# A decoder layer's projections with another order of loads, fold, keys and queries, and layer norm's last step on ScalarE

## The reference

```
m, v = mean(x), var(x);  xn = (x - m) / sqrt(v + 1e-5)
Q, K, V = xn @ Wq.T + bq, xn @ Wk.T + bk, xn @ Wv.T + bv      # 16 heads of 16
M[h] = shift_weights[h, g - f] for 0 <= g - f < 8, else 0
scores = (gt * (Q W_cross) K + (1 - gt) * Q (M K)) / 4,  gt = sigmoid(gate)
attn = softmax(causal(scores));  x += attn V @ Wo.T + bo
second: cross attention on ctx (4 x 77 x 256), keys ctx @ xWk, values ctx @ xWv
third: a gated feed-forward with integer weights, hidden size 768
```

## Time and profile before

| | us |
|---|---|
| runs, median (3 runs) | 1121.59 (1118.68 to 1123.11) |
| profiled execution | 1129.87 |
| its span | 1128.1 |
| PE busy | 1045.1 |
| DVE busy | 741.7 |
| ACT busy | 562.6 |
| POOL busy | 222.3 |
| mean granted clock of PE, as a share of full | 0.951 |

### The profile page before, as it was taken

How to read it: one execution, slowest core, us unless ns; L and a number is a source line. 1 busy time by engine, 2 the same in 40 slices (tenths; PEclk the granted TensorE clock), 3 DMA queues, 4 the chain that set the end, 5 groups by cost and what they waited for, 6 DMA issues and landing times. The chain is left out here.

```text
span 1128.1 us, 19085 instructions
## 1 busy us (share of the span) xinstructions
PE 1045.1 (93%) x7044; PEld 620.4 (55%) x7092; DVE 741.7 (66%) x1603; ACT 562.6 (50%) x1061; POOL 222.3 (20%) x199
## 2 busy tenths in 40 slices
PE   2888889999999999999999799899898899999997
PEld 2777434444444444444444366444443688888886
DVE  5999887777787778877885266555444555555552
ACT  1445146666666667666766458377655211111110
POOL 6545540000000000000000023201101133333331
PEclk9999779999999999999999899699968899999999
DMA  8259812333444444444400135687971211111101
GB/s 245 104 198 232 260 30 40 64 67 71 74 74 79 81 77 78 81 81 78 78 16 14 25 102 138 144 197 150 220 157 64 74 39 50 51 51 49 44 20 37
DMA packets 87827, 105.27 MB, mean 93 GB/s; under 512 B 14910, under 2 KB 76010, under 8 KB 86199
## 3 DMA queue, kind: packets, MB, share of 16 engines
q1 hardware_dynamic: 85239, 100.90, 38.4%
q10 hardware_dynamic: 2496, 3.16, 1.3%
HBM read 61.80 MB, written 37.06 MB: 88 GB/s over the span
## 5 line engine op out<-in xcount | busy, mean ns | idle before, releaser
L738 DVE TENSOR_REDUCE pm<-bank 128x1 f32<-128x512 f32 (+3 forms) x608 | 356.6, 653 | 87.5 <-PE bank L814 66.7
L786 ACT ACTIVATE prob<-bank 128x512 f32<-128x512 f32 (+1 forms) x608 | 317.4, 583 | 186.0 <-PE bank L830 99.1
L809 PE MATMUL bank<-stk,stq 96*128 96x512 bf16 (+3 forms) x768 | 227.4, 340 | 5.1 <-DVE pm L738 2.9
L826 PE MATMUL bank<-stq,stk 98*128 98x512 bf16 (+3 forms) x768 | 222.4, 330 | 2.6 <-ACT prob L786 0.5
L840 PE MATMUL bank<-prob,va 128*17 128x512 f32 (+3 forms) x1536 | 145.5, 497 | 2.5
L809 PEld LDWEIGHTS bank<-stk,stq 96*128 96x128 bf16 x768 | 68.8, 98 | 136.9 <-DVE pm L738 81.0
L1541 ACT ACTIVATE e_sg<-bank 128x512 f32<-128x512 f32 x48 | 28.7, 598 | 189.3 <-PE bank L135 189.3
L959 POOL TENSOR_TENSOR c_rstd<-c_ve,mhalf 128x4 f32<-128x4 f32 x8 | 8.1, 1011 | 504.9 <-DVE c_ve L128 504.9
L1296 ACT ACTIVATE xprob<-bank 80x512 f32<-80x512 f32 x128 | 72.5, 592 | 69.1 <-PE bank L1336 67.8
L826 PEld LDWEIGHTS bank<-stq,stk 98*128 98x128 bf16 x768 | 69.4, 99 | 44.9 <-ACT prob L786 9.2
L1258 DVE TENSOR_REDUCE xpm<-bank 128x4 f32<-128x320 f32 x128 | 59.0, 488 | 39.1 <-PE bank L1321 37.5
(11 more groups left out here) (172 smaller groups left out, 1403.8 us busy)
## 6 DMA issues: line engine op xcount, KB each, us to landing
qk<-a_parts SPq DMA_DIRECT2D x32, 384.0 KB, 4.4
od<-xu SPq DMA_DIRECT2D x16, 512.0 KB, 4.8
xq<-c_parts SPq DMA_DIRECT2D x16, 384.0 KB, 2.7
xstq<-xq SPq DMA_DIRECT2D x32, 192.0 KB, 4.6
stq<-qk SPq DMA_DIRECT2D x30, 192.0 KB, 4.0
stk<-qk SPq DMA_DIRECT2D x15, 384.0 KB, 6.5
vs<-a_vst SPq DMA_DIRECT2D x8, 544.0 KB, 4.7
oall<-u_out SPq DMA_DIRECT2D x64, 64.0 KB
```

Source lines behind the costliest of these rows:

```text
L738: nc.vector.tensor_reduce(pm[:, k, h0:h0 + hb, r], src[:, 0:hb * w].rearrange("p (h w) -> p h w", h=hb), AX, ALU.max).then_inc(s_mxe, 1)
L786: nc.scalar.activation(prob[:, U % NPS, 0:hb * n], bank[STB[U % NSB]][:, 0:hb * n], ACT.Exp).then_inc(s_ex, 1)
L809: mm = nc.tensor.matmul(dst[:, h * w:(h + 1) * w], stq[i][0:R, half, h0 + h, r * P:(r + 1) * P], stk[i][0:R, h0 + h, k0:k0 + w], start=(h ...
L826: mm = nc.tensor.matmul(dst[:, h * n:(h + 1) * n], stk[i][0:RM, h0 + h, kt * P:(kt + 1) * P], stq[i][0:RM, half, h0 + h, q0:q0 + n], start ...
```

## The change

Five things are moved:
- **Loads.** SP issues x of chunk 0 first, then the gates under a semaphore of their own (`s_gate`), then the other small ones, the context, and bk and bv behind it. ACT issues Wk and Wv ahead of Wq.
- **Before the first chunk.** DVE fills the constant rows of stk (from POOL) and takes the statistics of chunk 0 first, then builds A. PE turns chunk 0 first, then computes the context's products, each in its own bank, then the fold. POOL fills kp, does chunk 0's power, fills vx and takes the weights' low parts before the triangles.
- **Keys in front of queries.** The first pair of products is keys, the second queries, so Wq's low part is due at the third product. The order of the three parts and the place in `qk3` follow.
- **Layer norm's last step.** The mean is taken with its sign reversed, POOL multiplies it by rstd (`negm`), and ACT normalises as scale * x + bias. Its place on ACT is behind middle 3.
- **The bias fold** goes to a spare part of a fold's bank.

```diff
         def qkv_sync(sp):
-            sp.dma_start(wc[:], W_cross.rearrange("(t h) f g -> (h f) t g", t=KT)).then_inc(s_small, 16)
+            sp.dma_start(xres[:, 0], xv[0]).then_inc(ldx[0], 16)
+            for t in range(KT):
+                hs = slice(t * HP, (t + 1) * HP)
...
+                    sp.dma_start(gt[:, t:t + 1],
+                                 gate[hs].rearrange("(h a b) -> h a b", a=1, b=1).to_broadcast([HP, HD, 1])).then_inc(s_gate, 16)
             for t in range(KT):
                 hs = slice(t * HP, (t + 1) * HP)
                 sp.dma_start(sw[:, t, :], shift_w[hs, None, :].to_broadcast([HP, HD, MS])).then_inc(s_small, 16)
...
+            sp.dma_start(wc[:], W_cross.rearrange("(t h) f g -> (h f) t g", t=KT)).then_inc(s_small, 16)
...
-            sp.dma_start(xres[:, 0], xv[0]).then_inc(ldx[0], 16)
...
+            nc.gpsimd.memset(kp[:], 0.0).then_inc(s_con, 1)
+            power1(g, 0)
+            nc.gpsimd.memset(vx[:], 0.0).then_inc(s_con, 1)
+            g.wait_ge(s_con, 2)
+            nc.gpsimd.memset(vx[0:S2, :, :, HD:VW], 1.0).then_inc(s_con, 1)
+            weight_low(n_k, wk, 0)
+            weight_low(n_v, wv, 1)
...
-            power1(g, 0)
-            weight_low(n_k, wk, 0)
-            weight_low(n_v, wv, 1)
+            power1(g, 1)
...
-            self_constants(g, 0, 2)
-            power1(g, 1)
...
             nc.gpsimd.tensor_tensor(rstd[:, c % 2], ve[:, c % 2], mhalf[:], ALU.pow).then_inc(s_pow, 1)
+            g.wait_ge(s_pow, c + 1)
+            nc.gpsimd.tensor_tensor(negm[:, c % 2], mom[:, c % 2, 0], rstd[:, c % 2], ALU.mult).then_inc(s_nm, 1)
...
             nc.vector.memset(vst[:].rearrange("p u g j d h -> p (u g j) d h")[:, :, HD], 1.0)
+            for i in range(2):
+                nc.vector.memset(stk[i][R:RM], -1.0).then_inc(s_set, 1)
+            stats1(0)
             v.wait_ge(s_a, 1)
...
-            stats1(0)
-            normalise1(0)
-            for k in range(KT):
-                v.wait_ge(s_wqh, k + 1)
-                nc.vector.tensor_tensor(wq[:, 1, k], bank[FOLD[k]][:, 0:D], wq[:, 0, k].bitcast(F32),
-                                        ALU.subtract).then_inc(s_wl, 1)
             turned_low(0)
             stats1(1)
...
-            normalise1(1)
+            for k in range(KT):
+                v.wait_ge(s_wqh, k + 1)
+                nc.vector.tensor_tensor(wq[:, 1, k], bank[FOLD[k]][:, 0:D], wq[:, 0, k].bitcast(F32),
+                                        ALU.subtract).then_inc(s_wl, 1)
...
                 split(c, 2)
                 split(c, 3)
-                if c + 2 < NCH:
-                    normalise1(c + 2)
...
-            a.wait_ge(s_small, 16 * N_SMALL)
+            a.wait_ge(s_gate, 16 * KT)
             nc.scalar.activation(ge[:], gt[:], ACT.Exp, scale=-1.0).then_inc(s_a, 1)
+
+            def normalise1(c):
+                u = c % 2
+                a.wait_ge(s_nm, c + 1)
+                need(a, s_tr, KT * (c - 1))
+                for j in range(J):
+                    nc.scalar.activation(xn[:, u, j], xres[:, c, j], ACT.Identity, scale=rstd[:, u, j:j + 1],
+                                         bias=negm[:, u, j:j + 1]).then_inc(s_xn, 1)
+
+            normalise1(0)
...
+            a.wait_ge(s_fold, 2)
+            nc.scalar.activation(qkb[:, 1, :], FOLDB, ACT.Identity).then_inc(s_a, 1)
+            for k in range(KT):
+                nc.scalar.activation(wq[:, 0, k], bank[FOLD[k]][:, 0:D], ACT.Identity).then_inc(s_wqh, 1)
+            normalise1(1)
...
                 middle(c, 2)
                 middle(c, 3)
+                if c + 2 < NCH:
+                    normalise1(c + 2)
...
-                if i:
-                    t.wait_ge(s_kp, 1)
...
                     if c == 0 and n == KT:
-                        t.wait_ge(s_kl, 2)
-                    if c == 0 and n == 3:
-                        t.wait_ge(s_vx, 2)
-                    w_ = (wq, wk)[n // KT]
+                        t.wait_ge(s_wl, KT)
+                        t.wait_ge(s_a, 2)
+                    w_ = (wk, wq)[n // KT]
```

More of the change, by code:

```diff
@@ L167, in program @@
         rstd = sb(qkv, "a_rstd", [P, 2, J])
+        negm = sb(qkv, "a_negm", [P, 2, J])
         xn = sb(qkv, "a_xn", [P, 2, J, D])
@@ L179, in program @@
         ldx = sems("a_ldx", NCH)
+        s_gate = sem("a_gate")
         s_small = sem("a_small")
+        s_nm = sem("a_nm")
         s_wq = sem("a_wq")
@@ L216, in program @@
         TB, QKB, VB = (0, 1), (2, 3, 4, 5), (6, 7)
-        FOLD, CTXK, CTXV = (2, 3, 4), (5, 6), (7, 5)
-        N_SMALL = 2 + 2 * KT
+        FOLD, CTXK, CTXV = (4, 5), (6, 7), (2, 3)
+        FOLDB = bank[FOLD[1]][:, D:D + KT]
+        N_SMALL = 2 + KT
         def part_at(n, part):
-            return part if n < KT else 2 - part
+            return 2 - part if n < KT else part
         def qkv_sync(sp):
-            sp.dma_start(wc[:], W_cross.rearrange("(t h) f g -> (h f) t g", t=KT)).then_inc(s_small, 16)
+            sp.dma_start(xres[:, 0], xv[0]).then_inc(ldx[0], 16)
+            for t in range(KT):
+                hs = slice(t * HP, (t + 1) * HP)
+                with nc.allow_non_contiguous_dma(reason="gates on partitions, a few words"):
+                    sp.dma_start(gt[:, t:t + 1],
+                                 gate[hs].rearrange("(h a b) -> h a b", a=1, b=1).to_broadcast([HP, HD, 1])).then_inc(s_gate, 16)
             for t in range(KT):
@@ L240, in qkv_sync @@
             sp.dma_start(xwv[:], xWv.rearrange("(t p) n -> p t n", p=P)).then_inc(s_ctx, 16)
+            with nc.allow_non_contiguous_dma(reason="biases on partitions, a few hundred words"):
+                sp.dma_start(qkb[:, 0, :], bk.rearrange("(t p) -> p t", p=P)).then_inc(s_wk, 16)
+            sp.dma_start(bv_b[:], bv.rearrange("(a n) -> a n", a=1).to_broadcast([P, D])).then_inc(s_wv, 16)
             for c in range(2, NCH):
@@ L295, in weight_low @@
                 nc.gpsimd.tensor_tensor(w[:, 1], raw[:], w[:, 0].bitcast(F32), ALU.subtract).then_inc(s_kl, 1)
+            nc.gpsimd.memset(kp[:], 0.0).then_inc(s_con, 1)
[5 more added lines that the diff above has]
+            weight_low(n_v, wv, 1)
             nc.gpsimd.memset(trif[:], 0.0).then_inc(s_con, 1)
             nc.gpsimd.memset(self_[:], 0.0).then_inc(s_con, 1)
[L299 to L302, removed]
+            g.wait_ge(s_con, 5)
             nc.gpsimd.affine_select(out=trif[:, 0, :], in_=trif[:, 0, :], compare_op=ALU.is_ge, fill=NEG,
@@ L347, in stats1 @@
                 v.wait_ge(ldx[c], 16)
[L348 to L356, removed]
+                need(v, s_nm, c - 1)
+                moments(v, s_sum, c, xres[:, c], stat[:, c % 2], mom[:, c % 2], ve[:, c % 2], -1.0)
             def turned_low(c):
@@ L464, in turned @@
                     nc.scalar.activation(xnt[:, c % 2, 0, k], bank[TB[k]][:], ACT.Identity).then_inc(s_xh, 1)
[L466 to L470, removed]
             turned(0)
-            a.wait_ge(s_con, 5)
+            a.wait_ge(s_con, 3)
             for o in range(KT):
-                a.wait_ge(s_cx, 1 + o + 1)
+                a.wait_ge(s_cx, o + 1)
                 nc.scalar.activation(kp[:, o, 2, :, 0:S2],
@@ L525, in values @@
                 m.then_inc(s_vm, 1)
+            t.wait_ge(s_g, 8)
+            turn(0)
+            t.wait_ge(s_ctx, 16 * 3)
+            for o in range(KT):
+                for k in range(KT):
+                    m = nc.tensor.matmul(bank[CTXK[o]][:, 0:B * S2], xwk[:, k, o * P:(o + 1) * P], ctx[:, k],
+                                         start=(k == 0), stop=(k == KT - 1))
+                m.then_inc(s_cx, 1)
+            for i in range(2):
+                for bb in range(2):
+                    b = 2 * i + bb
+                    for k in range(KT):
+                        m = nc.tensor.matmul(bank[CTXV[i]][0:S2, bb * D:(bb + 1) * D], ctx[:, k, b * S2:(b + 1) * S2],
+                                             xwv[:, k], start=(k == 0), stop=(k == KT - 1))
+                m.then_inc(s_cx, 1)
             t.wait_ge(s_ab, KT)
@@ L535, in qkv_tensor @@
             for o in range(KT):
[L536 removed]
+                m = nc.tensor.matmul(FOLDB[:, o:o + 1], ablk[:, o, :], bq_c[:, o:o + 1],
                                      start=True, stop=True)
[L538 to L557 removed]
+            m.then_inc(s_fold, 1)
+            t.wait_ge(s_kl, 2)
+            t.wait_ge(s_vx, 2)
             for c in range(NCH):
```

32 lines of the change are left out of this document (4 added, 28 removed).

## The result

The changed kernel has a median of 1111.8 us in 7 runs (1108.05 to 1116.67), the kernel before beside it 1124.45 in 7 (1118.68 to 1145.06). The ratio is 0.988, 95% interval 0.985 to 0.991: 13.5 us less, between 10 and 17. The run of 1145.06 belongs to a slower state of the chip; without it the median before is 1123.78. On the 1121.59 that was shown the ratio gives 1108; predicted were 1106.1, in a range of 1100 to 1114. Saving and range were right; the sum held one error of up to 2 us and one of up to 3.

What follows compares the result with a forecast made beforehand. DVE was taken to bound the projection chunks, and bytes in the DMA queues their end. Prologue 6.2 us and shorter chunks made 15.5 us won at group 0's loads; off the shown median 1121.59 that gave 1106.1, range 1100 to 1114.

Steps and rivals of the forecast that it cites:

- The memsets: Prologue: DVE's two stk memsets before the statistics take 4.3 us each, 8.6 together, leaving DVE free at 9.7.
- The rival of fast memsets: Prologue: memsets take 1.7 us each, so x sets the start; 19.6 us off, 1102.0; chance 14%.
- x first is worth nothing by itself: Prologue: x, loaded first, lands between 4 and 9.5 us, under the memsets, so loading it first wins nothing.
- Statistics to the first turn: Prologue: statistics done at 11.9, GpSimd's power and negm at 13.2, ACT's normalising at 15.4, where PE's turn starts.
- The fold: Prologue: DVE's fold of the shifts is ready at 18.5 under context's products, or at 25.4 if stretched, costing 1 us.
- Chunk 0: End of prologue: ACT starts chunk 0 at 29.0 where it was 35.20, 6.2 us won.
- The chunk: Projections loop through ACT and DVE: 10.1 us per chunk in place of 11.5; group 0's loads at 69.4, 15.5 us won.
- The tail: End of projections: held by queued bytes, chunk 7 starts 33.0 us behind the loads, at 102.4, not the engines' 99.2.
- the rival: Tail not held by bytes: chunk 7 starts at 99.2, 18.7 us off, 1102.9; chance 8%.
- From there the order is as before ... and the barrier moves with the same queues: Behind chunk 7: DVE reaches the maxima 6.6 us later, at 109.0 for 124.49, and the barrier moves along.
- a stretch behind the maxima that differs: Sign against the forecast: any stretch behind the first maxima differing from before would show it wrong.
- The low clock: Slower rival: PE at 1.2 GHz through chunk 3, 36 us lost for 15.5 won, 1142; chance 4%.

Runs made afterwards that it cites:

- memset_late: Changed kernel with the two stk memsets moved from DVE to GpSimd, behind the low parts of chunks 0 and 1; 1112.97 us, ratio 0.989 to the kernel before.
- norm_on_vector: Changed kernel with layer norm's last step back on DVE from chunk 2 on; 1117.81 us, ratio 0.988 to the kernel before.
- group1_loads_last: Changed kernel with group 1's loads moved from behind chunk 4's stores to behind chunk 7's; 1103.14 us, ratio 0.984 to the kernel before.
- norm_alone: Kernel before with only layer norm's last step moved to ACT, chunk 1 normalised between high 1 and middle 0 of chunk 0; 1125.9 us, ratio 0.998.
- gpsimd_waits: Changed kernel; GpSimd waits for the first maxima cut before its memset, the second before its additions to xres; 1110.4 us, ratio 0.989 to the kernel before.
- two_parts: Changed kernel with group 1's loads last and GpSimd waiting for the first and third cut, memsets left on DVE; 1094.79 us, ratio 0.976.
- best_halves: Changed kernel with group 1's loads last, GpSimd waiting for first and third cut, stk memsets in halves on GpSimd behind chunks 0 to 3; 1098.74 us, ratio 0.978.
- x_seventh: Changed kernel with x of chunk 0 put back as the seventh of SP's DMAs; 1114.29 us in one run.
- memset_late_x_seventh: Changed kernel with stk memsets late on GpSimd and x of chunk 0 as SP's seventh DMA; 1120.96 us in one run.
- all_three: Changed kernel with memset_late, group1_loads_last and gpsimd_waits joined; 1107.03 us, ratio 0.986 to the kernel before.

## Why the prediction was right, and where it was not

1. **The memsets.** Predicted 4.3 us each. Shown are 3.47, and 0.8 us in front of each that the profile puts down to issue, 4.28 from start to start: DVE was free at 9.7, to the tenth. The Trainium skill ("VectorE: DVE Perf Modes", section "Zero memsets can be issued as uint32 (trn2)") has a cycle per element for a memset; these rows, 8.66 us for both, agree. The rival of fast memsets falls with it. The price came from the slope of another instruction, a reduction; that it fitted is in part luck, as nothing in the rows tied the two.
2. **x first is worth nothing by itself: wrong.** This step took the old landing of x, at most 9.5, as hidden. Put back into seventh place x lands at 11.6, behind the small loads: 1.9 us lost at the statistics, 1.5 at the loads. The sum was not hurt, as it needed only that x lands by 9.7 when loaded first; it lands at 5.96.
3. **Statistics to the first turn.** Predicted 11.9, 13.2, 15.4; GpSimd's power started at 12.11, ACT at 13.57, PE at 15.79. Each lies within 0.4 us.
4. **The fold.** Predicted ready at 18.5 or, stretched, at 25.4; it was ready at 20.3. The end I had named did occur in part: moving the weights' low parts on GpSimd put them beside the two products by the gates, 2.65 us instead of 0.47. It stayed hidden by 4 us of context products. In memset_late, where chunk 0 came earlier, the same two products took 3.14 us and stood in the chain that gave 2 of 3 us back.
5. **Chunk 0** at 28.19 for 29.0: the fold's products ran at twice the pace (1.05 us for eight, 2.08 before), on a PE that had no idle time before them.
6. **The chunk** at 10.03 for 10.1, and the loads at 69.33 for 69.4. The loop through ACT and DVE that the prediction added up fits as the bound, with 0.6 us of PE's wait a chunk; norm_on_vector shows that the 1.5 us a chunk are the normalising. That the loads fit to 0.1 us is luck: chunk 0 came 0.8 us early, the way from there to the loads took 41.1 for 40.4, and the same prologue put the loads anywhere from 68.95 to 70.13.
7. **The tail.** Held by bytes, as predicted: group1_loads_last shows it. Mis-sized twice. From the loads to chunk 7 it took 34.3 and 34.5 us (33.0 and 32.4 before), where the prediction had 33.0 and gave half a microsecond more for a denser queue; all variants of the changed kernel that load group 1 there need 34.3 to 34.6, whatever their prologue or loop, and norm_alone 34.1. Why these bytes need 1.3 to 2 us more stays open. And PE was ready at about 96.5, not 99.2: the estimate ran at the full chunk's 10 us, but chunk 6 has neither statistics nor normalising for a later chunk. So ACT's wait ahead of chunk 7 was 8.64 us, 7.1 of them beyond PE's end and not some 3, and moving those loads was worth 7, not the 3 that the rival put on it.
8. **"From there the order is as before ... and the barrier moves with the same queues": wrong by 3 us.** The order is, the instants aren't, and the prediction had named a stretch behind the maxima that differs as a sign that it is wrong. The barrier ended 14.75 us earlier, the first cut 14.2; before, the cut at 130.66 was over when GpSimd's memset started at 131.21, now they start at 116.44 and 116.46, and DVE's copy stands for 3.56 us. It puts 3.4 us into the first exp. By the third cut 2.3 are left or less (41.5 and 41.3 us behind the maxima, 39.2 and 40.7 before), because the kernel before had paid for a collision with the additions at its second cut, where two of DVE's small instructions took 2.27 and 2.26 us; the changed kernel has one of these.
9. **The low clock**, the rival on the slow side: the clock granted in the chunks was 1.00, and in the 21.5 us from the first maxima on 0.58 (0.56 before; the 0.68 shown for 104 to 126 takes in the end of chunk 7). It did not come in the changed kernel. The kernel before had some of it too, 0.79 from 70 to 78 us and 0.66 from 105 to 110, and in norm_alone it came for two short stretches and took part of the gain.

Sum by marks: 15.55 at the loads, less 1.35 in the tail, less 2.3 behind the maxima, is 11.9; in the second profiles 15.9, less 2.1, less 0.5, is 13.3. Their mean is 12.6.

## What to carry to other kernels

A stage whose end hangs on bytes returns what is won in it only if the bytes are fewer or stand elsewhere: look which transfers stand in front of the one that is waited for, and whether they are needed at that moment. When work moves in time, check what else runs on the shared resource at the new instant, small instructions included; an order between two engines that no semaphore keeps is luck. A part that wins in every chunk (norm_alone) can lose half of it in front of the first chunk, so try parts from both sides, and read such a run's own prologue before concluding that it needs another part.

## What the runs showed of the hardware

**A small copy can wait for a whole memset.** DVE's CAST of 128x16 took 3.56 us beside a GpSimd memset of 3.51 that starts with it, in the changed kernel and its second profile, 3.55 in norm_alone, and 0.17 in gpsimd_waits, where the memset came later. A multiplication by a scalar, 128x4, took 3.47 (norm_alone, 27.23), and two SBUF inputs of 128x16 took 2.26 beside an addition on GpSimd (before, 149.85). The page "SBUF — State Buffer" of the Trainium skill, section "Who interferes with whom", says that GpSimd and a DVE instruction in a mode that uses both ports, casts and scalar products among them, take a shared pair in turns, the later one blocked for the whole of the other, and that two SBUF inputs do the same against a GpSimd instruction that reads. These rows agree; only which came first can't be read at the CAST, whose row starts 0.02 us ahead of the memset's. What I had not expected is that 16 columns suffice.

**The same stage takes another time in each execution.** Cross attention, which no edit here touches, took these times from its first exp to the first gate of the feed-forward, with the clock granted in it (1.00 is 2.4 GHz):

| | us | clock |
|---|---|---|
| before, twice | 164.9, 163.9 | 0.87, 0.87 |
| changed, twice | 158.5, 161.4 | 0.91, 0.90 |
| two_parts | 158.8 | 0.91 |
| gpsimd_waits | 167.6 | 0.86 |
| best_halves | 171.9 | 0.83 |

That is 13 us from one profiled execution to another, as much as the whole change gives, and it goes with the clock (x_seventh had 161.9 at 0.88, norm_on_vector 160.9 at 0.90, memset_late_x_seventh 165.8 at 0.86). Of the 9.2 us by which the two spans shown differ beyond 12.6, it holds 6.4. Whether an edit can shift the clock of a later stage stays open: one profile per kernel can't tell. A part of a change is better judged by a mark of the stage that it touches, with the mark's own scatter in mind. And a mark is not yet time: at the fourth cut gpsimd_waits is 4.4 us ahead of the changed kernel and all_three 9.7, but their medians are only 1.4 and 4.8 us lower.
